# Gated graph layers on one core: dense superblocks of 16 quads whose sums land in two spans of 256 columns

## The chip, the cores and the metric

The kernel runs on one core of a Trainium2 chip. The metric is the time of one execution on the device, in microseconds (us); the lower, the better. The kernel before was run three times: median 3903.62 us, from 3901.79 to 3904.91. A fourth execution was profiled.

## What is computed

A graph of 12500 nodes with 128 features and 212500 edges, sorted by destination, goes through three gated graph layers:

```python
h = x @ lin_w.T + lin_b            # x here: relu of the layer norm of the input
for i in range(3):
    m = h @ weight[i]
    agg = segment_sum(m[src], dst, n_nodes)
    h = gru_cell(agg, h, w_ih, w_hh, b_ih, b_hh)
return x_in + h
```

The sum over edges is the expensive part: each of 212500 edges adds a row of 128 numbers of `m` to the row of its destination.

## The kernel before, in words

**Edges.** 512 consecutive edges are a quad: 4 chunks (`QC`) of 128. There are 416 quads. As the edges are sorted by destination, a quad touches few nodes: its destinations lie in a window of `W` = 36 nodes from its lowest one. Sums are kept transposed in `aggT`, features on the partitions and nodes along the columns, so a quad adds 36 columns at a column known only on the chip. VectorE makes a plan first (lines 971 to 1050): the lowest node of every quad, the edges' distances to it, and flags that say whether every edge lies in its window. All engines wait for the flags and then take one of two written orders of work. With these inputs it is the first (`TILES_AT`, `AHEAD`).

**Two ways to sum.** The quads are cut in 16 superblocks of `SQ` = 26 consecutive quads. In each layer a superblock's last `GQ` = 12 quads are gathered and its first `DQ` = 14 are dense.
- *Gathered* (a step is two quads): GpSimd issues eight indirect DMAs, one a chunk (line 565), that bring 128 message rows each, in three bf16 pieces, into a ring of 4 steps. TensorE multiplies them with onehots that VectorE makes (24 small matmuls, line 827), and VectorE adds the two windows into `aggT` (line 1174), its columns from registers loaded from the plan.
- *Dense*: no message is gathered. For a superblock there is a matrix of counts, source nodes by columns: how many edges go from a source to each of a quad's 36 window columns. Its product with all messages of the 12544 source nodes (98 blocks of 128) gives all 14 windows at once, 14 x 36 = 504 columns of PSUM (lines 846 to 865). The messages are split by VectorE in two fp32r halves (lines 1283, 1285), so there are 98 x 2 matmuls a superblock. The counts come from HBM as bytes, a slice of 7 blocks per DMA (line 509), and ScalarE widens them (line 682). Work is cut in units of 2, 2 and 3 blocks (`UNITS`), 42 a superblock; two slices of six units in all are buffered (`UBUF`).

**The counts** are made once, in layer 0, where the first `KG` = 7 superblocks are gathered whole (91 steps, `TURN`). For every one of 16 x 14 = 224 dense quads VectorE makes onehots of its sources (lines 1241, 1249), and in 7 rounds of 14 blocks (`ROUNDS`) TensorE counts with 4 matmuls (line 842) into one of three banks of PSUM. ScalarE writes the bank as bytes into `quad_counts` (`evacuate`, line 709), and SP stores 7 quads, half a superblock, with 7 DMAs (line 515), each as soon as the last quad's round has left PSUM. The next superblock's same half waits for these stores. After all stores SP loads the first counts and messages (lines 509, 501). From step 91 on layer 0 sums its other 9 superblocks half dense, half gathered.

**Order.** Each engine runs the steps of a layer in a written order (`layer_steps`): 145, 96 and 96 steps. On TensorE a step is: the sums of the gathered rows, the next messages of a tile (256 nodes), the counting rounds or seven dense units (`STEP_UNITS`), and the gates of a tile when all its sums are in (`TILES_AT`). On VectorE: the two adds of the step, onehots, parts of tiles, then in turn the splitting of units and, once a superblock's last unit is multiplied, `add_superblock`: 14 adds of 36 columns (line 1188), each waiting on the one before, seven register loads before each seven. The gathers of the next layer wait until all messages of a layer are stored; dense units of its first parts are done ahead, in the steps after a layer's last gather.

The change touches also the loads (`counts_in`), the layout of the counts in HBM, and what TensorE waits for (`s_dadd`: the adds of a superblock two back, in whose bank it writes).

## Time and profile before

| | |
|---|---|
| median of 3 runs | 3903.62 us |
| profiled execution: its own time | 3896.86 us |
| profiled execution: span, first to last instruction | 3895.0 us |
| mean granted TensorE clock | 0.952 |
| TensorE matmuls, busy | 3452.6 us, 89% |
| ScalarE, busy | 3020.0 us, 78% |
| VectorE, busy | 2870.7 us, 74% |
| GpSimd, busy | 2756.7 us, 71% |
| DMA | 758.66 MB, 195 GB/s |

In the rows PE is TensorE's matmuls, PEld its weight loads, DVE VectorE, ACT ScalarE, POOL GpSimd, SP the sync engine; an engine's name with q is its sequencer. L565 is line 565 of the kernel before. The span falls in stages: the plan and the first messages up to about 157 us, gathers with counting up to about 1130, a gap until the first counts are back at about 1195, the dense part of layer 0 until 1818, layer 1 until 2892, layer 2 until the end. Granted clock is the share of 2.4 GHz that TensorE was given: 1.0, or 0.5 (1.2 GHz), and means between them over a stretch.

### The profile page before, as it was taken

The page shows a single profiled execution, that of the slowest core. Times are in us where ns is not written, and L with a number is a line of the kernel's source. Part 1 is how long each engine was busy: PE and PEld are TensorE (multiplying, and loading weights), DVE is VectorE, ACT ScalarE, POOL GpSimd, SP SyncE. Part 2 cuts the span into 40 slices and gives each one's busy share as a digit, 9 for nine tenths or more (in the row PEclk, how much of TensorE's full clock was granted, in tenths as well). Part 3 has the DMA queues.
Part 4 walks back from the last instruction along what each step waited for, and adds up shares of the span by engine and source line. Part 5 has one row for each costly group of instructions (what it writes and reads, how often), then busy time and mean ns, then how long its engine had stood idle before and what let it go on. Part 6 is the DMA issues. An engine that isn't in the chain of part 4 may idle for free.

```text
span 3895.0 us, 74412 instructions
## 1 busy us (share of the span) xinstructions
PE 3452.6 (89%) x25008; PEld 2729.5 (70%) x25009; DVE 2870.7 (74%) x8189; ACT 3020.0 (78%) x4231; POOL 2756.7 (71%) x2758
## 2 busy tenths in 40 slices
PE   6289999999979999987999999999979999999996
PEld 4167666766667777765777777777757777777775
DVE  7478888888867777765777777777757777777774
ACT  4179888888878888776788788787857887878783
POOL 4777777777777777733777777777737777777776
PEclk8699999999989999998999999999989999999998
DMA  8346566565577666665666666666756666666664
GB/s 274 108 152 216 187 197 208 185 200 196 180 240 235 192 198 198 191 183 169 194 204 199 198 202 207 192 205 191 227 159 191 205 197 196 204 194 202 194 201 121
DMA packets 461502, 758.66 MB, mean 195 GB/s; under 512 B 66760, under 2 KB 337864, under 8 KB 461128
## 3 DMA queue, kind: packets, MB, share of 16 engines
q1 hardware_dynamic: 216472, 411.54, 33.0%
q0 software_dynamic: 129408, 265.20, 24.6%
q10 hardware_dynamic: 115248, 77.10, 6.4%
q8 instruction: 213, 3.49, 0.4%
q14 instruction: 161, 1.32, 0.1%
HBM read 578.11 MB, written 175.47 MB: 193 GB/s over the span
## 4 chain that ended last, share of the span: by engine, by line
PE 43%; POOL 23%; DVE 11%; issue 10%; ACT 7%; DMA 4%; DVEq 2%; ACTq 0%; SPq 0%; POOLq 0%
POOL ring_region L565 23%; PE psum L860 18%; PE psum L842 16%; ACT wide_counts L682 4%; DVE quad_onehots L1249 2%; PE psum L815 2%; PE psum L827 2%; DMA states<-temps 2%; DVE aggT L1188 2%; DVEq L1140 2%; DVE message_halves L1285 1%; PE psum L785 1%; PE psum L786 1%; PE psum L787 1%; ACT quad_counts L709 1%
## 5 line engine op out<-in xcount | busy, mean ns | idle before, releaser
L565 POOL DMA_INDIRECT ring_region<-messages,edge_src x2696 | 2702.7, 1002 | 1048.7 <-issue 804.2
L860 PE MATMUL psum<-wide_counts,message_halves 128*128 128x504 f32 x8036 | 1988.3, 404 | 149.7 <-DVE message_halves L1285 129.7
L682 ACT CAST wide_counts<-messages_region 128x1008 fp32r<-128x1008 uint8 x1722 | 1880.7, 1170 | 257.9 <-PE psum L860 202.6
L860 PEld LDWEIGHTS psum<-wide_counts,message_halves 128*128 128x128 f32 x8036 | 1517.0, 192 | 516.5 <-ACT wide_counts L682 111.9
L1285 DVE TENSOR_TENSOR message_halves<-messages_region,message_halves 128x256 fp32r<-128x256 f32 x1722 | 810.9, 471 | 59.3
L842 PE MATMUL psum<-quad_onehots,block_onehots 128*128 128x238 bf16 (+2 forms) x6272 | 768.3, 272 | 60.6 <-ACT quad_counts L709 42.4
L709 ACT CAST quad_counts<-psum 128x504 uint8<-128x504 f32 x1568 | 770.6, 643 | 28.5 <-PE psum L842 26.5
L842 PEld LDWEIGHTS psum<-quad_onehots,block_onehots 128*128 128x128 bf16 x6272 | 539.7, 100 | 276.4 <-issue 47.6
L1283 DVE CAST message_halves<-messages_region 128x256 fp32r<-128x256 f32 x1722 | 656.7, 381 | 64.0 <-PE psum L860 35.2
L1249 DVE TENSOR_SCALAR quad_onehots<-iota_quad,count_keys 128x1666 bf16<-128x1666 f16 (+2 forms) x896 | 528.3, 652 | 0.0
L827 PEld LDWEIGHTS psum<-onehot,ring_region 128*128 128x128 bf16 x8088 | 243.4, 96 | 187.2 <-issue 160.3
L827 PE MATMUL psum<-onehot,ring_region 128*128 128x36 bf16 x8088 | 258.2, 179 | 129.6 <-DMA ring_region<-messages,edge_src 122.2
L1174 DVE TENSOR_TENSOR aggT<-aggT,psum 128x36 f32 x674 | 128.3, 190 | 227.6 <-PE psum L827 100.1
L1241 DVE TENSOR_SCALAR block_onehots<-iota_block,count_keys 128x128 bf16<-128x128 bf16 x896 | 171.6, 274 | 108.1 <-PE psum L842 107.3
L1188 DVE TENSOR_TENSOR aggT<-aggT,psum 128x36 f32 x574 | 110.7, 193 | 182.3 <-issue 88.9
L627 ACT ACTIVATE temps<-psum,small 128x256 f32<-128x256 f32 x147 | 69.2, 471 | 211.7 <-PE psum L815 211.2
L815 PE MATMUL psum<-aggT,wih 128*128 128x256 f32 x882 | 219.4, 386 | 10.6 <-DVE aggT L1188 10.6
L1217 DVE SCALAR_TENSOR_TENSOR temps<-psum,small,temps 128x256 f32<-128x256 f32 x147 | 70.6, 480 | 196.7 <-ACT temps L627 188.7
L815 PEld LDWEIGHTS psum<-aggT,wih 128*128 128x128 f32 x882 | 172.1, 195 | 36.2 <-issue 11.4
L637 ACT ACTIVATE temps<-temps,small 128x256 f32<-128x256 f32 x147 | 75.1, 511 | 127.3 <-DVE temps L1219 127.1
L1149 DVE TENSOR_TENSOR onehot<-iota_block,edge_rel 128x288 bf16<-128x288 bf16 x337 | 152.1, 452 | 1.7 <-DVE count_keys L1070 0.9
L665 ACT CAST pieces_out<-temps 128x256 bf16<-128x256 f32 x98 | 41.7, 426 | 139.1 <-DVE temps L1196 139.1
(104 smaller groups left out, 1529.3 us busy)
## 6 DMA issues: line engine op xcount, KB each, us to landing
messages_region<-counts SPq DMA_DIRECT2D x574, 441.0 KB
counts<-quad_counts SPq DMA_DIRECT2D x224, 441.0 KB
ring_region<-messages,edge_src POOLq DMA_INDIRECT x2696
messages<-pieces_out ACTq DMA_DIRECT2D x98, 192.0 KB
messages_region<-plain SPq DMA_DIRECT2D x21, 896.0 KB, 7.6
temps<-states ACTq DMA_DIRECT2D x98, 128.0 KB
states<-temps ACTq DMA_DIRECT2D x98, 128.0 KB
plain<-temps ACTq DMA_DIRECT2D x98, 128.0 KB
```

The costliest lines, as they stand in the source:

```text
L565: nc.gpsimd.indirect_dma_start(out=rows[:, n % RING, h * QC + c, :], out_offset=None, in_=messages[layer], in_offset=bass.IndirectOffsetOn ...
L682: nc.scalar.copy(wide_counts[:, v % UBUF, :, cols], stage[v % ABUF][:, :, cols]).then_inc(s_wide, 1)
L709: nc.scalar.copy(quad_counts[half][:, 2 * i:2 * i + 2, j % HQ, :], psum[:, COUNT_BANKS[r % 3], 0:RW].rearrange("p (s w) -> p s w", w=SLW)) ...
L815: nc.tensor.matmul(bank, wih[:, gate * P:(gate + 1) * P], nodes, start=alone, stop=True, skip_group_check=not alone).then_inc(s_gate, 1)
L827: mm = nc.tensor.matmul(window(n, h), rows[:, n % RING, i, k * P:(k + 1) * P], onehot[:, n % 3, i, :], start=(c == 0 and k == 0), stop=(c ...
L842: mm = nc.tensor.matmul(by_block[:, :, SUBLOW[c]:SUBLOW[c] + SUBW[c]], blocks_oh[j % 2][:, c, :], x_round, start=(k == 0), stop=True, skip ...
L860: mm = nc.tensor.matmul(psum[:, 6 + kg % 2, 0:DQ * W], halves[:, v % UBUF, b % HB, half * P:(half + 1) * P], wide_counts[:, v % UBUF, :, c ...
L1188: nc.vector.tensor_tensor(cols, cols, psum[:, 6 + kg % 2, q * W:(q + 1) * W], ALU.add).then_inc(s_dadd, 1)
L1241: made = nc.vector.tensor_scalar(blocks_oh[j % 2][:, c, :], iota_lo[:], los[:, col:col + 1], None, ALU.is_equal)
L1249: made = nc.vector.tensor_scalar(xs[j % 2][c], iota_x[:, 0:NB * SUBW[c]], keys[:, col:col + 1], -float(SUBLOW[c]), ALU.subtract, ALU.is_equal)
L1283: nc.vector.tensor_copy(high, whole).then_inc(s_high, 1)
L1285: nc.vector.tensor_tensor(low, whole, high.bitcast(F32), ALU.subtract).then_inc(s_low, 1)
```

## The change

Superblocks have 28 quads, 16 of them dense; there are 15, the last one short of 4 gathered quads (`CUT` = 2 steps). The 16 dense quads of a superblock are two halves of 8. The 8 windows of a half share one span of `WW` = 256 columns that starts at the lowest node of its first quad, so a dense matmul has 2 x 256 columns, and a superblock's sums are added with two adds of 256 columns.

For that the counts of a quad are put in place when they leave PSUM: ScalarE writes them into `half_counts` (98 blocks of 264 bytes) at the quad's offset in the span. The offsets are a third row of the plan, loaded into registers of ScalarE eight at a time. Windows overlap: a quad leaves its column 0 alone when it isn't the first of a half, as this node may be shared with the quad before, and an extra round (two matmuls of 98 columns, one of them with `shared_onehots`) counts that column for both quads; ScalarE copies it in as 98 single bytes. VectorE clears the tail of a half beforehand. The plan gets new conditions (gaps between quads, offsets, edges beyond the next quad) and one more onehot key per quad (`shared_keys`). Stores wait for a whole half. `blocks_oh` gets a third buffer.

```diff
-SQ = 26
-DQ = 14
+SQ = 28
+DQ = 16
 GQ = SQ - DQ
 HB = 7
 HQ = DQ // 2
-SLW = HB * W
+WW = 256
+WS = 264
+LAST_FROM, LAST_TO = WS - 2 * W, WS - W
 RW = 2 * HB * W
...
 SUBW = (12, 19, 17, 17)
+SUBFROM = (0, 1, 11, 19)
...
-FIRST_DENSE = 9 / 16
+FIRST_DENSE = 8 / 15
...
-    NSB = NQ // SQ
-    AGG = NODES + W
-    assert NPAD % (PTN * PRO) == 0 and NQ % SQ == 0 and out.shape[0] % TN == 0 and NB % (2 * HB) == 0
+    NSB = -(-NQ // SQ)
+    QUADS = NSB * SQ
...
-    STEPS = [TURN + KD * GSB, G_STEPS, G_STEPS]
-    STEP0 = [0, STEPS[0], STEPS[0] + G_STEPS]
+    STEPS = [TURN + KD * GSB - CUT, G_STEPS - CUT, G_STEPS - CUT]
+    STEP0 = [0, STEPS[0], STEPS[0] + STEPS[1]]
     TOTAL = sum(STEPS)
     BUILDS = NSB * DQ
-    BUILD_ROUNDS = BUILDS * ROUNDS
+    COUNTED = [(j, i) for j in range(BUILDS) for i in range(ROUNDS + (j % HQ > 0))]
+    COUNTED_AT = {round_of: e for e, round_of in enumerate(COUNTED)}
+    COUNTED_BY = [max(e for e, (quad, _) in enumerate(COUNTED) if quad == j) + 1 for j in range(BUILDS)]
...
+                whole = s == STEPS[layer] - 1 and (not ahead or layer == LAYERS - 1)
+                now = end if whole else min(block_of(unit_of(d) + STEP_UNITS), max(d, end))
...
+            half_counts_t = shared("half_counts", [P, 2, NB, WS], U8)
-            blocks_oh_t = shared("block_onehots", [P, 2, QC, P], BF16)
+            blocks_oh_t = shared("block_onehots", [P, 3, QC, P], BF16)
+            shared_oh_t = shared("shared_onehots", [P, 2, NB], BF16)
...
-        wide_counts = sb("wide_counts", [P, UBUF, DQ, HB * W], F32R)
+        wide_counts = sb("wide_counts", [P, UBUF, HB, 2, WW], F32R)
...
-        stage = [byte_at(region, ST0 + b * AB, DQ * SLW, U8).rearrange("p (q w) -> p q w", w=SLW)
+        stage = [byte_at(region, ST0 + b * AB, AB, U8).rearrange("p (h b w) -> p b h w", h=2, w=WS)
...
+        counts_tail = [half_counts_t[:, half].bitcast(F32)[:, :, LAST_TO // 4:WS // 4] for half in range(2)]
...
-                sp.dma_start(stage[v % ABUF], counts[k, j]).then_inc(s_al[v % ABUF], 16)
+                sp.dma_start(stage[v % ABUF].rearrange("p b h w -> p h b w"), counts[k, j]).then_inc(s_al[v % ABUF], 16)
 
             for g in range(BUILDS // HQ):
                 k, half = BUILD_ORDER[g // 2], g % 2
+                sp.wait_ge(s_ev, COUNTED_BY[HQ * g + HQ - 1])
                 for i in range(ROUNDS):
-                    sp.wait_ge(s_ev, ROUNDS * (HQ * g + HQ - 1) + i + 1)
-                    sp.dma_start(counts[k, 2 * i:2 * i + 2, :, HQ * half:HQ * (half + 1), :].rearrange(
-                        "s p q w -> p s (q w)"), quad_counts[half][:, 2 * i:2 * i + 2].rearrange(
-                        "p s q w -> p s (q w)")).then_inc(s_ast[half], 16)
+                    sp.dma_start(counts[k, 2 * i:2 * i + 2, :, half].rearrange("s p b w -> p s (b w)"),
+                                 half_counts[half][:, 2 * HB * i:2 * HB * (i + 1), :].rearrange(
+                                     "p (s b) w -> p s (b w)", b=HB)).then_inc(s_ast[half], 16)
...
-                cols = slice(*(W * b for b in UNITS[w % UN]))
+                here = slice(*UNITS[w % UN])
                 if w % UN == 0:
                     act.wait_ge(s_al[v % ABUF], 16 * (v // ABUF + 1))
                 unit_used(act, w - UBUF * UN)
-                nc.scalar.copy(wide_counts[:, v % UBUF, :, cols], stage[v % ABUF][:, :, cols]).then_inc(s_wide, 1)
+                nc.scalar.copy(wide_counts[:, v % UBUF, here], stage[v % ABUF][:, here, :, 0:WW]).then_inc(s_wide, 1)
...
+                j, i = COUNTED[e]
                 k, half = j // DQ, j % DQ // HQ
-                act.wait_ge(s_bld, r + 1)
-                if k and j % HQ == 0 and i == 0:
-                    act.wait_ge(s_ast[half], 16 * ROUNDS * k)
-                nc.scalar.copy(quad_counts[half][:, 2 * i:2 * i + 2, j % HQ, :],
-                               psum[:, COUNT_BANKS[r % 3], 0:RW].rearrange("p (s w) -> p s w", w=SLW)).then_inc(s_ev, 1)
+                if j % HQ == 0 and i == 0:
+                    first = DQ * BUILD_ORDER[k] + HQ * half
+                    _, values = nc.values_load_multi_w_load_instructions(
+                        plan[0:1, 2, first:first + HQ], [mybir.EngineType.Activation], min_val=0, max_val=LAST_TO,
+                        skip_runtime_bounds_check_because=ON_CHIP)
+                    columns.update((j + q, value) for q, value in enumerate(values))
+                    act.wait_ge(s_tail, j // HQ + 1)
+                    if k:
+                        act.wait_ge(s_ast[half], 16 * ROUNDS * k)
+                act.wait_ge(s_bld, e + 1)
+                counted = psum[:, COUNT_BANKS[e % 3], :]
+                if j % HQ:
+                    act.wait_ge(s_ev, COUNTED_AT[j - 1, min(i, ROUNDS - 1)] + 1)
+                if i < ROUNDS:
+                    own = 1 if j % HQ else 0
+                    nc.scalar.copy(half_counts[half][:, 2 * HB * i:2 * HB * (i + 1), own:WS][
+                                       :, :, bass.ds(columns[j], W - own)],
+                                   counted[:, 0:RW].rearrange("p (b w) -> p b w", w=W)[:, :, own:W]).then_inc(s_ev, 1)
+                else:
+                    nc.scalar.copy(half_counts[half][:, :, bass.ds(columns[j], 1)],
...
+                if i == ROUNDS:
+                    pe.wait_ge(s_xshare, j - j // HQ)
+                    first_column = xs[j % 2][0].rearrange("p (b w) -> p b w", w=SUBW[0])[:, :, 0]
+                    nc.tensor.matmul(counted[:, 0:NB], blocks_oh[j % 3][:, 0, :], first_column, start=True, stop=False)
+                    nc.tensor.matmul(counted[:, 0:NB], blocks_oh[(j - 1) % 3][:, QC - 1, :], shared_oh[j % 2],
+                                     start=False, stop=True).then_inc(s_bld, 1)
+                    return
...
-                    pe.wait_ge(s_dadd, DQ * (kg - 1))
-                cols = slice((b % HB) * W, (b % HB + 1) * W)
+                    pe.wait_ge(s_dadd, 2 * (kg - 1))
                 for half in range(HALVES):
-                    mm = nc.tensor.matmul(psum[:, 6 + kg % 2, 0:DQ * W],
+                    mm = nc.tensor.matmul(psum[:, 6 + kg % 2, 0:2 * WW],
                                           halves[:, v % UBUF, b % HB, half * P:(half + 1) * P],
-                                          wide_counts[:, v % UBUF, :, cols], start=(b == 0 and half == 0),
+                                          wide_counts[:, v % UBUF, b % HB].rearrange("p h w -> p (h w)"),
+                                          start=(b == 0 and half == 0),
                                           stop=(b == NB - 1 and half == HALVES - 1))
...
+            dense_low = dense_quads(lowest_all)
+            nc.vector.memset(gap[:, NQ - 1:NQ], float(FAR)).then_inc(s_win, 1)
+            nc.vector.tensor_tensor(gap[:, 0:NQ - 1], lowest[:, 1:NQ], lowest[:, 0:NQ - 1], ALU.subtract
+                                    ).then_inc(s_win, 1)
+            for half in range(2):
+                quads = slice(HQ * half, HQ * (half + 1))
+                nc.vector.tensor_tensor(offsets[:, :, quads], dense_low[:, :, quads],
+                                        dense_low[:, :, HQ * half:HQ * half + 1].to_broadcast([P, NSB, HQ]),
+                                        ALU.subtract).then_inc(s_win, 1)
...
+            nc.vector.tensor_tensor(beyond_c[:, :, 0:QC - 1], by_quad[:, :, 0:QC - 1],
+                                    limit_of.to_broadcast([P, NQ, QC - 1]), ALU.is_ge).then_inc(s_win, 1)
...
+            nc.vector.tensor_tensor(outside, outside, beyond, ALU.max).then_inc(s_win, 1)
...
+            near_next = chunk_of(edge_rel[:], QC - 1, SQ)[:, :, 0:DQ - 1]
+            nc.vector.tensor_tensor(shared_keys[:, :, 1:DQ], near_next, dense_quads(gap_all)[:, :, 0:DQ - 1], ALU.is_equal
+                                    ).then_inc(s_keys, 1)
...
-                    count = DQ // 2
-                    values = lows_of(SQ * k + half * count, count)
-                    for j in range(count):
-                        q = half * count + j
-                        cols = aggT[:, bass.ds(values[j], W)]
-                        if kg or q:
-                            dve.wait_ge(s_dadd, DQ * kg + q)
-                        nc.vector.tensor_tensor(cols, cols, psum[:, 6 + kg % 2, q * W:(q + 1) * W], ALU.add
-                                                ).then_inc(s_dadd, 1)
+                    value, = lows_of(SQ * k + HQ * half, 1)
+                    cols = aggT[:, bass.ds(value, WW)]
+                    if kg or half:
+                        dve.wait_ge(s_dadd, 2 * kg + half)
+                    nc.vector.tensor_tensor(cols, cols, psum[:, 6 + kg % 2, WW * half:WW * (half + 1)], ALU.add
+                                            ).then_inc(s_dadd, 1)
...
+                k, half = j // DQ, j % DQ // HQ
+                if j % HQ == 0:
+                    if k:
+                        dve.wait_ge(s_ast[half], 16 * ROUNDS * k)
+                    nc.vector.memset(counts_tail[half], 0.0).then_inc(s_tail, 1)
                 block_onehot(j)
+                if j % HQ:
+                    nc.vector.tensor_scalar(shared_oh[j % 2], iota_hi[:, 0:NB], shared_keys[:, BUILD_ORDER[k], j % DQ:j % DQ + 1],
+                                            None, ALU.is_equal).then_inc(s_xshare, 1)
```

## Rows read from the trace of the kernel before

**Rows 1.** The page: busy time of the engines, and the chain by engine.
```profile
PE 3452.6 (89%) x25008; PEld 2729.5 (70%) x25009; DVE 2870.7 (74%) x8189; ACT 3020.0 (78%) x4231; POOL 2756.7 (71%) x2758
...
PE 43%; POOL 23%; DVE 11%; issue 10%; ACT 7%; DMA 4%; DVEq 2%; ACTq 0%; SPq 0%; POOLq 0%
```

**Rows 2.** Costliest groups, dense stretches of layer 0, 1 (two), 2: busy, mean ns | idle.
```profile
L860 PE MATMUL psum<-wide_counts,message_halves 128*128 128x504 f32 x1593 | 392.2, 402 | 38.8 <-DVE message_halves L1285 38.7
...
L565 POOL DMA_INDIRECT ring_region<-messages,edge_src x673 | 667.5, 992 | 221.2 <-issue 200.1 <-PE psum L827 21.1
L860 PE MATMUL psum<-wide_counts,message_halves 128*128 128x504 f32 x2660 | 667.1, 408 | 53.0 <-DVE message_halves L1285 52.7
...
L860 PE MATMUL psum<-wide_counts,message_halves 128*128 128x504 f32 x2980 | 727.4, 400 | 29.3 <-DVE message_halves L1285 27.9 <-ACT wide_counts L682 1.3
```

**Rows 3.** Stretches: length, busy PE, PEld, DVE, ACT, POOL, clock, DMA, GB/s.
```profile
205.00:1125.00 920.00, 859.42 (x8494) 639.52 (x8493) 777.06 (x2163) 810.64 (x1689) 699.06 (x680) 0.99 0.60 193
1195.00:1730.00 535.00, 496.15 (x3153) 401.32 (x3152) 390.85 (x1112) 428.55 (x509) 366.49 (x370) 0.96 0.66 193
...
1892.00:2780.00 888.00, 833.25 (x5284) 676.17 (x5281) 652.07 (x1866) 718.57 (x857) 667.12 (x673) 0.96 0.67 199
...
2895.00:3840.00 945.00, 895.68 (x5794) 726.53 (x5794) 711.59 (x2025) 755.28 (x771) 722.87 (x730) 0.99 0.66 196
```

**Rows 4.** Counting: a piece of the chain (start, us), and costliest groups.
```profile
383.57 9.02 PE psum L842 x76
...
L709 ACT CAST quad_counts<-psum 128x504 uint8<-128x504 f32 x1552 | 762.4, 644 | 27.7 <-PE psum L842 25.9
L842 PE MATMUL psum<-quad_onehots,block_onehots 128*128 128x266 bf16 (+1 forms) x6214 | 760.1, 272 | 60.6 <-ACT quad_counts L709 42.4 <-DVE quad_onehots L1249 17.8
```

**Rows 5.** Timeline of layer 1 (start, us, what), and a stretch as in rows 3.
```profile
2141.32 7.65 PE L860 MATMUL psum<-wide_counts,message_halves 128*128 128x504 f32 x32
...
2162.76 2.14 DVE L1188 TENSOR_TENSOR aggT<-aggT,psum 128x36 f32 x7 [1.37 <-PE psum L860]
...
2166.66 2.13 DVE L1188 TENSOR_TENSOR aggT<-aggT,psum 128x36 f32 x7 [1.76 <-issue]
...
2169.62 3.38 PE L860 MATMUL psum<-wide_counts,message_halves 128*128 128x504 f32 x8 [4.20 <-DVE message_halves L1285]
...
2169.60:2176.00 6.40, 5.76 (x19) 4.24 (x20) 5.45 (x16) 4.44 (x5) 4.87 (x6) 0.73 0.46 132
```

**Rows 6.** The plan on VectorE: groups, then the timeline after 120 us.
```profile
L1017 DVE TENSOR_TENSOR messages_region<-messages_region 128x416 f32<-128x416 f32 x4 | 3.4, 889 | 0.1
...
L998 DVE TENSOR_TENSOR edge_rel<-edge_rel,messages_region 128x1664 f32<-128x1664 f32 x1 | 1.9, 1867 | 0.0
...
123.44 1.36 POOL L565 DMA_INDIRECT ring_region<-messages,edge_src  x1 [0.21 <-issue]
...
157.17 0.52 DVE L1174 TENSOR_TENSOR aggT<-aggT,psum 128x36 f32 x2 [0.73 <-PE psum L827]
...
172.95 0.52 DVE L1174 TENSOR_TENSOR aggT<-aggT,psum 128x36 f32 x2 [9.14 <-PE psum L827]
```

**Rows 7.** Operations of 256 columns from PSUM, over the span.
```profile
L1219 DVE TENSOR_TENSOR temps<-temps,psum 128x256 f32<-128x256 f32 x147 | 61.8, 421 | 5.1
...
L655 ACT COPY temps<-psum 128x256 f32<-128x256 f32 x98 | 35.2, 359 | 11.2 <-PE psum L798 11.2
```

**Rows 8.** The last stores of counts: their issue, and the last one's landing.
```profile
1131.31 6.88 SPq L515 DMA_DIRECT2D counts<-quad_counts  x7
...
1136.98 7.46 DMA counts<-quad_counts
```

**Rows 9.** TensorE at the ends of layers 0 and 1.
```profile
1748.05 2.90 PE L815 MATMUL psum<-aggT,wih 128*128 128x256 f32 x6 [9.49 <-DVE aggT L1188]
...
1818.06 0.88 PE L827 MATMUL psum<-onehot,ring_region 128*128 128x36 bf16 x24 [17.71 <-DMA ring_region<-messages,edge_src]
...
2892.25 0.88 PE L827 MATMUL psum<-onehot,ring_region 128*128 128x36 bf16 x24 [16.36 <-DMA ring_region<-messages,edge_src]
```

143 lines of the change are left out of this document (104 added, 39 removed).

## The prediction, made before the change was run

> **What bounds the kernel now.** I read the engines' busy shares first, then the chain of waits, then the span cut at the kernel's stages, then each stage's costliest lines. TensorE is busiest, and the chain is TensorE 43% and GpSimd 23% [rows 1]: two engines share the bound. GpSimd does nothing but issue gathers, one per 0.99 + 0.30 us [rows 2], so a step of eight costs 10.3 us and six steps (one superblock) 61.9 us, whatever the others do.
>
> By stage [rows 3] (a superblock is 196 dense matmuls):
> - 205 to 1125: counting. 224 quads in 920 us, 4.11 us a quad. Per quad TensorE is busy 3.84 us, ScalarE 3.62, VectorE 3.47: TensorE bounds and ScalarE is close behind, and TensorE's largest wait is for ScalarE's evacuation [rows 4].
> - 1195 to 1730: layer 0's dense part, 1593 matmuls are 8.13 superblocks: 65.8 us each. Layer 1, from 1892 us on, 2660 are 13.57: 65.4 us each. Layer 2, 2980 are 15.2: 62.2 us each [rows 2, 3]. Layer 2 therefore already goes at the gathers' pace. Layers 0 and 1 don't, and the reason is in the waits: TensorE waits for VectorE's halves 38.7, 52.7 and 27.9 us in the three stretches.
> - One such wait from close by [rows 5]: VectorE makes 14 adds of 36 columns, each waiting for the one before, in two groups with register loads between, from 2162.76 to 2168.79: 6.0 us in which it splits no messages. TensorE runs out and idles 4.2 us. Then the granted clock of the next 6.4 us is 0.73: between the levels 2.4 and 1.2 GHz, part of it at the lower, where a dense matmul takes 0.42 us (8 in 3.38) against 0.24 (32 in 7.65). The granted clock over the stretch is 0.96 in layers 0 and 1, 0.99 in layer 2 [rows 3], that is 2.6 us lost per superblock in the first two and 0.6 in the last.
>
> **The change, part by part.** From the constants: 16 superblocks of 26 quads become 15 of 28, the number of gathered quads in one stays 12. The last superblock is short by 4 gathered quads (2 steps). Steps go from 145, 96, 96 to 144, 88, 88; dense superblocks over all layers from 41 to 38; counted quads from 224 to 240, their rounds from 1568 to 1680, with 210 small extra rounds for the shared column.
>
> *Plan.* Some 18 more VectorE instructions stand before the flags. By rows of like size [rows 6]: one over 1664 elements 1.9 us, one over three quarters of them 1.4, four over strided 416 at 0.89, and a dozen over fewer elements, each below that, which I estimate at 3 together: 10 us. The three on the shared keys add 1. TensorE sums nothing until then, but the gathers run: the first is issued at 123.4, the ring of four steps is full 32 gathers of 1.3 us later, at 165, and the adds soon come at the gathers' pace (the one at 172.95 after 9.1 us of waiting for sums). The first add moves 11 us, from 157 to 168, so the gathers stall some 3 us. **+3**; without that cover it would be +11, and nothing less than 0.
>
> *Counting, TensorE.* A quad gets two matmuls of 98 columns for 7 of 8 quads. Nineteen rounds (76 matmuls of 227 columns on average) take 9.02 us, 0.119 each [rows 4]; 98 columns save 129/2.4 = 54 ns: 0.065 each, 0.13 a quad. Ends: 0, hidden in ScalarE's time, and 0.24. Busy becomes 3.97 us a quad.
>
> *Counting, ScalarE.* The evacuation of 504 columns lasts 644 ns and, overlapping, costs 0.49 each. It now writes 14 runs of 35 bytes at a column held in a register, and waits for its own earlier result. No such write is in the trace; the nearest is VectorE's add at a register's column that waits for the one before, 0.305 us apart, under 0.49 [rows 5]. So I take 0.49 (lower end 0.48 for 14 columns fewer; upper end 0.644, no overlap). The extra copy of 98 columns: from 644 ns at 504 and 359 at 256 [rows 4, 7], 1.15 ns a column, 0.18 us; upper end a whole 0.49. Register loads, eight a half: seven took 1.76 us on VectorE [rows 5], so 0.25 us a quad; lower end 0 if they run ahead. Together 3.62 + 0.18 + 0.25 = 4.05 us a quad: ScalarE passes TensorE.
>
> *Counting, VectorE.* One onehot of 98 columns (0.2) and, per 8 quads, a clearing of 882 elements (0.9 us, 0.11 a quad): 3.78 us a quad. It stays under the others and costs nothing while they are slower; uncovered it would be 0.3 a quad. The clearing waits for the stores of the same half; behind it in VectorE's queue are adds and onehots. It comes two quads ahead of use, some 26 us after that half's last count, and the last stores of a half landed 7.5 us after issue [rows 8]: covered.
>
> *Sum.* A quad took 0.27 us more than its busiest engine; with two engines nearly level I allow 0.30: 4.35 us, 240 quads 1044 us against 920: **+124**. Ends: loads hidden, 4.10, +64; every evacuation unoverlapped, under the rivals.
>
> *The turn.* Seven stores now wait in SP's queue for the whole half, where six went out while the last quad was still counted; behind them are all the loads. The seven were issued over 6.9 us and the last landed 7.5 later, and the first load followed [rows 8]. Nearly all of those 6.9 us come after the last count now: **+6**, between 0 and 12.
>
> *Dense superblocks.* 14 serial adds with their loads become 2 of 256 columns: an add of 256 columns with PSUM 0.42 us [rows 7], with its load 0.3 more, 1.4 us instead of 6 to 7. TensorE has six units in hand then (14 blocks, 28 matmuls, 6.7 us), so the wait goes, and with it most of the clock's fall. Per superblock: stall 4.8 us in layer 0 and 3.9 in layer 1, of which I take 3.2 to 4.0; clock 2.1; against it 196 matmuls 8 columns wider, 196 x 3.3 ns = 0.65, and 0.2 more of a tile, of the 11 us that sums and tiles take on TensorE per superblock (895.7 less 727.4 over 15.2 in layer 2), at most 0.9. TensorE's need falls to 61 us, level with the gathers' 61.9. Two engines level don't meet exactly: 63. Widening grows by 1.6%, on ScalarE, which is busy 81% of layer 1 [rows 3], beside TensorE. The tiles, the loads (532 of 473 KB for 574 of 441 KB) and the gathers are as before.
> - Layer 0: one superblock fewer, 7.13 at 63 = 449 for 535, -86; the layer's last tiles waited 9.5 us for the last adds [rows 9], now 3: -6; two gather steps fewer, 1 us of sums each: -2. **-94**.
> - Layer 1, 1818 to 2892 [rows 9]: 1074 = 16 x 65.4 + 28. Now 88 steps, 14.67 superblocks at 63 = 924, + 28, + 10 since 33 dense blocks (15.7 us, a third hidden by the wait for the next gathers) stand beside the last two tiles. 962: **-112**.
> - Layer 2: 1003 = 16 x 62.2 + 8. The gathers' pace stays: 14.67 x 62.2 = 912, + 8, + 3 for one more tile at the end: **-80**.
>
> Sum: 3 + 124 + 6 - 94 - 112 - 80 = **-153**. Against the profiled execution (span 3895.0, its own time 3896.9) this gives a span of 3742 and a time of 3744. The median of the three runs is 3903.6, 6.8 above it: **3751 us**, -3.9%.
>
> **The rivals.**
> *R1, the evacuation becomes the bound (slower).* If writes at a register's column in short runs, or the new wait on ScalarE's own semaphore, keep evacuations from overlapping, each costs its 644 ns: 4.51 + 0.18 + 0.25 + 0.18 = 5.12 us of ScalarE a quad, with 0.30 5.42, 240 quads 1300, 256 more than forecast: 4007 us. It decides from 0.583 us an evacuation on (153 us / 240 = 0.64 a quad). For it: ScalarE is 94% as busy as TensorE already, and layer 0 alone pays. Against: the wait is for a result seven evacuations old, and the register-addressed adds pass at 0.305.
> *R2, the one-column copies are dear.* They write 98 single bytes 264 apart and TensorE reads a column 12 elements apart. If a copy costs what an evacuation of 504 does, 0.31 more x 210 = 65 us: 3816. For it: nothing in the trace writes so thinly. Against: the copies are few.
> The Trainium skill (SBUF — State Buffer, Door 1) speaks for R2: SBUF has 16-byte cachelines and each access that crosses to a new line pays a penalty. It gives no price for ScalarE, and no run here shows one.
> *R3, another wait takes the place.* The stall and the clock's loss stay in other clothes (ScalarE's widening, 81% busy in layer 1 [rows 3], or late gathers), and only the count of superblocks pays: layer 0 7.13 x 65.8 = 469, -66 - 8; layer 1 14.67 x 65.4 + 38 = 997, -77; layer 2 -80. -231 + 133 = -98: 3806.
> *R4, the plan refuses.* If the new conditions on gaps and offsets failed for these node numbers, the flags would send all engines to the order with tiles last. Sums and tiles take TensorE 168 us in layer 2 [rows 2, 3], now among the dense work; alone after the steps they would add up to that in each layer: up to 4250. Destinations are sorted and quads 30 nodes wide, which fits 256 columns for 8.
>
> **Chances and range.** Forecast 0.57, R2 0.15, R3 0.16, R1 0.11, R4 0.01. About 0.2% is what a measurement here can tell from no change (the three runs span 0.08%). R2 and R3 with other shortfalls reach no change in 0.03. So faster 0.85, within 0.2% 0.03, slower 0.12. Low end: loads hidden, 3751 - 60, near 3695. High end: R2 and R3 together, 3871. R1 and R4 are left out.
>
> **What the profile would show.** Gathers 2560; dense matmuls 7448 at 0.24; adds of 256 columns 76; TensorE's wait for message halves under 30 us over the span (129.7 now) and the granted clock 0.98 or more in layer 1. Counting lasts some 1045 us with ScalarE over 90% busy in it, evacuations near 0.49 apart. Layer 1 and 2 take about 962 and 923 us. I am wrong if an evacuation costs 0.58 or more, if TensorE in layer 1 waits as long for something else, or if layer 2 isn't shorter by 80.

## The result, and the profile after

The changed kernel takes **3806.20 us** (median of four runs, 3801.6 to 3813.78) where the kernel before took 3904.26 on the same chip: a ratio of 0.9749, 95% interval 0.9737 to 0.9761, so 2.5% faster. The forecast was 3751, -3.9%, with a range from 3695 to 3871. The direction held; 55 us of the 153 did not come.

The page of the changed kernel, busy time by engine and the chain of waits, stands beside [rows 1]:

```profile
PE 3361.6 (88%) x24880; PEld 2652.7 (70%) x24881; DVE 2801.6 (74%) x7778; ACT 3044.4 (80%) x4427; POOL 2663.4 (70%) x2622
...
POOL 35%; PE 23%; issue 15%; ACT 15%; DVE 6%; DMA 4%; ACTq 1%; DVEq 0%; SPq 0%; POOLq 0%
```

Over the whole span PE, POOL and DVE do less, since there are fewer superblocks. ScalarE does more, in a shorter span, and its share of the chain went from 7% to 15%. TensorE's share fell from 43% to 23% and GpSimd's rose from 23% to 35% [rows 1]: the gathers now lead the chain.

The costliest groups of the page (line, engine, operation, tiles and shape, count | busy, mean ns | idle before it and what ended it):

```profile
L600 POOL DMA_INDIRECT ring_region<-messages,edge_src x2560 | 2609.2, 1019 | 1037.5 <-issue 764.2
L717 ACT CAST wide_counts<-messages_region 128x1024 fp32r<-128x1024 uint8 (+1 forms) x1596 | 1762.0, 1185 | 188.5 <-PE psum L920 155.1
L920 PE MATMUL psum<-wide_counts,message_halves 128*128 128x512 f32 x7448 | 1794.4, 398 | 70.3 <-DVE message_halves L1406 50.5
...
L903 PE MATMUL psum<-quad_onehots,block_onehots 128*128 128x266 bf16 (+1 forms) x6720 | 844.7, 272 | 104.2 <-ACT half_counts L758 63.8
L758 ACT CAST half_counts<-psum 128x490 f32 (+1 forms) x1680 | 846.9, 594 | 64.6 <-PE psum L903 40.2
L903 PEld LDWEIGHTS psum<-quad_onehots,block_onehots 128*128 128x128 bf16 x6720 | 576.4, 100 | 359.5 <-issue 137.0
...
L1354 DVE TENSOR_SCALAR block_onehots<-iota_block,count_keys 128x128 bf16<-128x128 bf16 x960 | 183.6, 271 | 137.9 <-PE psum L896 101.4
...
L762 ACT CAST half_counts<-psum 128x98 f32 x210 | 128.1, 610 | 0.0
```

Gathers (2560) and dense matmuls (7448) are as counted, and TensorE's wait for message halves is 50.5 us for 129.7. New is the last row: L762 is the one-column copy, **610 ns** for 98 bytes, as long as an evacuation of 490. And L903's weight loads stand 137 us for "issue", time for which the profile names no releaser; run 4 looks into a part of it.

The stretches of the changed kernel, as in [rows 3] (length, busy PE, PEld, DVE, ACT, POOL, granted clock, DMA share, GB/s): counting, then the dense parts of layers 0, 1 and 2.

```profile
206.00:1300.00 1094.00, 989.97 (x9550) 715.58 (x9551) 884.71 (x2568) 958.17 (x2018) 787.39 (x736) 0.99 0.52 167
1372.00:1800.00 428.00, 407.28 (x2681) 335.01 (x2680) 318.93 (x867) 367.69 (x441) 307.63 (x308) 1.00 0.71 209
1898.00:2814.00 916.00, 866.96 (x5678) 712.62 (x5675) 679.55 (x1826) 780.37 (x926) 693.87 (x695) 0.99 0.72 213
2872.00:3740.00 868.00, 824.79 (x5352) 679.96 (x5349) 641.48 (x1710) 701.07 (x716) 664.20 (x669) 0.98 0.68 202
```

The clock of layers 0 and 1 rose from 0.96 to 1.00 and 0.99. In the counting stretch TensorE is busy 90% and ScalarE 88% (forecast: over 90%): neither of the two is saturated.

To compare stage by stage I cut both spans at the starts of VectorE's adds of gathered steps, which every kernel here has (us; in brackets us per step):

| stage | before | after | difference | forecast |
|---|---|---|---|---|
| to the add of step 6 | 202.9 | 206.1 | +3 | +3 |
| counting, to two steps before the turn | 931.3 | 1104.1 | **+173** | +124 |
| turn, six steps | 62.6 | 62.6 | 0 | +6 |
| layer 0, dense steps | 535.3 (10.92) | 427.9 (10.44) | -107 | |
| layer 0's last add to layer 1's first | 87.0 | 97.7 | +11 | -94 with the line above |
| layer 1, steps | 1037.6 (10.92) | 915.6 (10.53) | -122 | |
| its last add to layer 2's first | 36.6 | 58.2 | **+22** | -112 with the line above |
| layer 2, steps | 986.4 (10.38) | 904.5 (10.40) | -82 | |
| end | 15.4 | 25.2 | +10 | -80 with the line above |
| span | 3895.0 | 3802.1 | -93 | -153 |

The dense stages did what was forecast, within 3 to 12 us each (layer 0 -97, layer 1 -100, layer 2 -72). Four fifths of the shortfall of 60 us of span (49) are in the counting; 12 more are at the turn from layer 1 to layer 2.

### The profile page after: what moved, and what is told of

It is laid out like the page before. It is cut to its first block, busy times and chain, and to the rows that moved or that the text cites. A ratio compares the mean times of both kernels' runs of the same rounds, so it can differ in the third digit from the quotient of the medians.

```text
span 3802.1 us, 76920 instructions
## 1 busy us (share of the span) xinstructions
PE 3361.6 (88%) x24880; PEld 2652.7 (70%) x24881; DVE 2801.6 (74%) x7778; ACT 3044.4 (80%) x4427; POOL 2663.4 (70%) x2622
## 4 chain that ended last, share of the span: by engine, by line
POOL 35%; PE 23%; issue 15%; ACT 15%; DVE 6%; DMA 4%; ACTq 1%; DVEq 0%; SPq 0%; POOLq 0%
POOL ring_region L600 34%; PE psum L903 16%; ACT wide_counts L717 10%; ACT half_counts L758 3%; DMA states<-temps 2%; DVE quad_onehots L1370 2%; PE psum L920 2%; PE psum L880 1%; PE psum L868 1%; DVE block_onehots L1354 1%; PE psum L811 1%; DVE temps L1330 1%; DMA messages_region<-counts 1%; PE psum L804 0%; ACTq L745 0%
## 5 line engine op out<-in xcount | busy, mean ns | idle before, releaser
L717 ACT CAST wide_counts<-messages_region 128x1024 fp32r<-128x1024 uint8 (+1 forms) x1596 | 1762.0, 1185 | 188.5 <-PE psum L920 155.1
L920 PE MATMUL psum<-wide_counts,message_halves 128*128 128x512 f32 x7448 | 1794.4, 398 | 70.3 <-DVE message_halves L1406 50.5
L920 PEld LDWEIGHTS psum<-wide_counts,message_halves 128*128 128x128 f32 x7448 | 1397.6, 191 | 374.8 <-ACT wide_counts L717 90.0
L903 PE MATMUL psum<-quad_onehots,block_onehots 128*128 128x266 bf16 (+1 forms) x6720 | 844.7, 272 | 104.2 <-ACT half_counts L758 63.8
L758 ACT CAST half_counts<-psum 128x490 f32 (+1 forms) x1680 | 846.9, 594 | 64.6 <-PE psum L903 40.2
L903 PEld LDWEIGHTS psum<-quad_onehots,block_onehots 128*128 128x128 bf16 x6720 | 576.4, 100 | 359.5 <-issue 137.0
L1406 DVE TENSOR_TENSOR message_halves<-messages_region,message_halves 128x256 fp32r<-128x256 f32 (+1 forms) x1596 | 751.0, 471 | 55.0
L1404 DVE CAST message_halves<-messages_region 128x256 fp32r<-128x256 f32 (+1 forms) x1596 | 611.4, 383 | 114.1 <-PE psum L920 75.7
L1370 DVE TENSOR_SCALAR quad_onehots<-iota_quad,count_keys 128x1176 bf16<-128x1176 f16 x960 | 560.7, 645 | 0.0
L1290 DVE TENSOR_TENSOR aggT<-aggT,psum 128x36 f32 x640 | 122.2, 191 | 216.4 <-PE psum L880 147.8
L762 ACT CAST half_counts<-psum 128x98 f32 x210 | 128.1, 610 | 0.0
```

The costliest lines, as they stand in the source:

```text
L717: nc.scalar.copy(wide_counts[:, v % UBUF, here], stage[v % ABUF][:, here, :, 0:WW]).then_inc(s_wide, 1)
L758: nc.scalar.copy(half_counts[half][:, 2 * HB * i:2 * HB * (i + 1), own:WS][:, :, bass.ds(columns[j], W - own)], counted[:, 0:RW].rearrange ...
L903: mm = nc.tensor.matmul(by_block[:, :, SUBLOW[c]:SUBLOW[c] + SUBW[c]], blocks_oh[j % 3][:, c, :], x_round, start=(k == 0), stop=True, skip ...
L920: mm = nc.tensor.matmul(psum[:, 6 + kg % 2, 0:2 * WW], halves[:, v % UBUF, b % HB, half * P:(half + 1) * P], wide_counts[:, v % UBUF, b % ...
L1370: made = nc.vector.tensor_scalar(xs[j % 2][c], iota_x[:, 0:NB * SUBW[c]], keys[:, col:col + 1], -float(SUBLOW[c]), ALU.subtract, ALU.is_equal)
L1404: nc.vector.tensor_copy(high, whole).then_inc(s_high, 1)
```

## Experiments

Every kernel ran with the kernel before on the same chip, three rounds and more. The ratios are to that kernel; the edits are to the changed kernel, or to the folded one where this is said.

**1. Registers taken out.** ScalarE's columns are constants, the 240 register loads go. The counts are put at 30 columns a quad instead of where they belong.

```diff
-                    _, values = nc.values_load_multi_w_load_instructions(...)
-                    columns.update((j + q, value) for q, value in enumerate(values))
+                    columns.update((j + q, 30 * q) for q in range(HQ))
...
-                                       :, :, bass.ds(columns[j], W - own)],
+                                       :, :, columns[j]:columns[j] + W - own],
...
```

> The kernel after, but ScalarE writes every quad at a constant column (30 per quad) instead of the plan's: no register loads on ScalarE and no register in the address. Counts stand up to some columns off their place, so the sums are not the reference's; the work is the same. Theory A (the counting lost its 49 us to the one-column rounds, not to registers): the eight loads a half are seen as some 17 us of idle, the time falls by 10 to 25 us to 3780-3796, evacuations stay 0.48 us apart. Rival B (writes at a register's column are slow): the spacing falls to 0.42-0.46 us and the time by 60 us or more, below 3746.

3770.31 us, ratio 0.9661 (0.9642 to 0.9681): 36 us less. Counting 1071.8 for 1104.1; evacuations start 471 ns apart for 479. More than theory A wrote down, and the spacing didn't fall as B wanted. The traces show one part of it: with a column from a register an evacuation starts 97 ns after TensorE's signal that its round is done, with a constant one 23 ns (medians). What costs more, the load or the address, is taken up in runs 8 to 10.

**2. The copy made cheap.** The one-column copy moves a single byte instead of 98; the other counts of the first columns are left out.

```diff
-                    nc.scalar.copy(half_counts[half][:, :, bass.ds(columns[j], 1)],
-                                   counted[:, 0:NB].unsqueeze(2)).then_inc(s_ev, 1)
+                    nc.scalar.copy(half_counts[half][:, 0:1, bass.ds(columns[j], 1)],
+                                   counted[:, 0:1].unsqueeze(2)).then_inc(s_ev, 1)
```

> The kernel after, but the copy of the shared column moves 1 element instead of 98 single bytes 264 apart; the rounds on TensorE stay. 97 of 98 blocks keep no count in the shared columns. Theory A1 (each single byte is dear, 4 to 5 ns): from this copy's start to the next evacuation's start goes from 0.48 to 0.1-0.25 us, ScalarE is freed of 50-75 us, and the time falls by 20 to 45 us, since TensorE's own 0.52 us per extra round stays. Rival A2 (the cost is fixed, whatever is copied): the spacing stays above 0.4 us and the time within 10 us of 3806.

3809.42 us, ratio 0.9748 (0.9726 to 0.9770): the time of the changed kernel. The copy did become cheap. The groups on ScalarE from 206 to 1240 us, and under them the stretch itself and ScalarE's longest wait in it, of this kernel:

```profile
L762 ACT CAST half_counts<-psum 128x1 f32 x195 | 35.2, 180 | 0.0
...
206.00:1240.00 1034.00, 933.36 (x8992) 685.83 (x8991) 833.29 (x2414) 843.57 (x1902) 716.02 (x694) 0.98 0.52 165
...
ACT half_counts L758 <- PE psum L903: 96.5, 244, 2.4
```

and of the changed kernel:

```profile
206.00:1240.00 1034.00, 935.26 (x9033) 675.52 (x9034) 837.66 (x2433) 907.46 (x1911) 746.49 (x697) 0.99 0.52 167
...
ACT half_counts L758 <- PE psum L903: 38.6, 65, 1.9
```

ScalarE is busy 64 us less and waits 58 us longer for TensorE: what it saved it waits. From the copy's start to the next evacuation's start are 480 ns as before, so A1's gain didn't come although the copy fell to 180 ns, as A1 had it. As long as the extra round stands on TensorE, the bytes of the copy are not what the counting goes by. So rival R2's mechanism falls, though its time (3816) was near.

**3. The serial adds put back.** Sixteen adds of 32 columns a superblock, each waiting on the one before, in place of two of 256 (the sums land at 32 columns a quad from the half's lowest node).

```diff
-                    value, = lows_of(SQ * k + HQ * half, 1)
-                    cols = aggT[:, bass.ds(value, WW)]
-                    if kg or half:
-                        dve.wait_ge(s_dadd, 2 * kg + half)
-                    nc.vector.tensor_tensor(cols, cols, psum[:, 6 + kg % 2, WW * half:WW * (half + 1)], ALU.add
-                                            ).then_inc(s_dadd, 1)
+                    values = lows_of(SQ * k + HQ * half, HQ)
+                    for j in range(HQ):
+                        q = HQ * half + j
+                        cols = aggT[:, 32 * j:AGG][:, bass.ds(values[0], 32)]
+                        if kg or q:
+                            dve.wait_ge(s_dadd, DQ * kg + q)
+                        nc.vector.tensor_tensor(cols, cols, psum[:, 6 + kg % 2, 32 * q:32 * (q + 1)], ALU.add
+                                                ).then_inc(s_dadd, 1)
```

> The kernel after, but a superblock's sums are added by 16 serial adds of 32 columns, with eight register loads before each eight, as the kernel before did with 14 of 36; same sums. Theory C (the dense stages gained by the stall and the clock that these adds cost, beside the fewer superblocks): TensorE's wait for message halves comes back to 100 us or more over the span from 50, the granted clock in layer 1 falls from 0.99 to 0.96, a superblock in layers 0 and 1 goes from 62.9 to 65.5 us or more, and the time rises by 50 to 90 us to 3856-3896. Rival D (only the smaller number of superblocks paid): within 15 us of 3806.

3865.52 us, ratio 0.9901 (0.9884 to 0.9917): 59 us more, three fifths of all that the change won. Per step, layer 0 10.98 for 10.44, layer 1 10.92 for 10.53, layer 2 10.38 for 10.40. Layer 1, dense matmuls and the stretch, of this kernel:

```profile
L920 PE MATMUL psum<-wide_counts,message_halves 128*128 128x512 f32 x2683 | 661.3, 403 | 54.9 <-DVE message_halves L1408 54.1 <-ACT wide_counts L717 0.8
...
1898.00:2814.00 916.00, 832.25 (x5343) 678.59 (x5342) 674.23 (x1932) 742.94 (x885) 682.42 (x684) 0.96 0.69 203
```

and the same group of the changed kernel:

```profile
L920 PE MATMUL psum<-wide_counts,message_halves 128*128 128x512 f32 x2847 | 685.1, 397 | 26.9 <-DVE message_halves L1406 26.9
```

With the adds back the wait for halves doubles (over the whole span it is 96.1 us for 50.5, a little under the 100 of theory C), the clock is 0.96 as before [rows 3], and 164 fewer matmuls get done in the same 916 us. Layer 2 doesn't change: it goes at the gathers' pace either way.

**4. The shared column folded in.** Instead of an extra round of two matmuls of 98 columns and a copy, each of the seven rounds adds the neighbour's share of its own 14 first columns with a fifth matmul of 14 columns, and the evacuation writes all 36 columns. Nothing of the counts is left out.

```diff
-    COUNTED = [(j, i) for j in range(BUILDS) for i in range(ROUNDS + (j % HQ > 0))]
+    COUNTED = [(j, i) for j in range(BUILDS) for i in range(ROUNDS)]
...
-                    own = 1 if j % HQ else 0
+                    own = 0
...
+                if j % HQ:
+                    mm = nc.tensor.matmul(by_block[:, :, 0], blocks_oh[(j - 1) % 3][:, QC - 1, :],
+                                          shared_oh[j % 2][:, 2 * HB * i:2 * HB * (i + 1)],
+                                          start=False, stop=True, skip_group_check=True)
                 mm.then_inc(s_bld, 1)
```

> The kernel after with the extra round folded in: in each of a quad's 7 rounds a fifth matmul of 14 columns adds the previous quad's shared node into column 0 in PSUM, ScalarE writes all 36 columns, and there is no separate round and no one-column copy. Theory A (the extra round costs ScalarE 0.49 and TensorE 0.52 us a quad): the counting stage goes from 1104 us to 1010-1050 and the time falls by 50 to 95 us to 3711-3756. Rival E (the counting stage is held by VectorE's onehots or the gathers): the stage stays above 1085 us and the time within 20 us of 3806.

3749.55 us, ratio 0.9606 (0.9590 to 0.9622): **57 us** less than the changed kernel, counting 1053.9 for 1104.1. The timeline of the changed kernel shows the price. TensorE in it, two quads (start, length, line, operation, count):

```profile
350.73 0.33 PE L895 MATMUL psum<-quad_onehots,block_onehots 128*128 128x98 bf16 x1
350.88 0.22 PE L896 MATMUL psum<-shared_onehots,block_onehots 128*128 128x98 bf16 x1
351.26 3.42 PE L903 MATMUL psum<-quad_onehots,block_onehots 128*128 128x266 bf16 x28
354.52 0.33 PE L895 MATMUL psum<-quad_onehots,block_onehots 128*128 128x98 bf16 x1
354.68 0.23 PE L896 MATMUL psum<-shared_onehots,block_onehots 128*128 128x98 bf16 x1
```

From L895 to L896 are 0.15 us, from L896 to the next round's first matmul 0.38 (medians over some 170 quads 0.155 and 0.362; between two matmuls of a round 0.111). An extra round takes TensorE 0.52 us from start to start.

The 0.36 are a wait for ScalarE. Ahead of each round TensorE waits (line 890) until the bank of three rounds before is emptied. The same place in the chain of waits, and another such place in the timeline:

```profile
350.49 0.63 ACT half_counts L758
351.12 0.14 issue
351.26 1.80 PE psum L903 x14
...
1301.66 0.22 PE L896 MATMUL psum<-shared_onehots,block_onehots 128*128 128x98 bf16 x1
1302.03 3.43 PE L903 MATMUL psum<-quad_onehots,block_onehots 128*128 128x266 bf16 x28 [0.15 <-ACT half_counts L758]
```

Of 168 extra rounds with a counting round right behind them, 28 have no such wait on record, and there the next round starts after 0.065 us. In 133 of the other 140 it starts 56 or 57 ns after the record of the wait ends, and an evacuation ended the wait. ScalarE in turn starts most evacuations 97 ns after a round of TensorE has ended (median), and gives the copy a whole slot of 0.48 (the median from L762 to the next L758, and the same from one L758 to the next). So the banks go round in a ring in which each engine waits for the other, and the extra round is one more turn of it. The bank that TensorE waits for behind an extra round is that of an evacuation and not the copy's, which fits with run 2 having won nothing. No run relieves TensorE alone, so its share and the copy's aren't told apart.

**5. No extra round at all.** Only the first two edits of run 4: the neighbour's share of a first column is left out.

> The changed kernel without the 210 extra rounds: the share that a quad's neighbour adds to its first column is left out, each quad evacuates all its columns itself. Theory A: an extra round cost TensorE 0.52 us start to start (0.123 + 0.155 + 0.362 less one ordinary matmul start of 0.12), 210 of them 109 us, and all of it was on the path: counting 1104 to 995, time 3697 (3680 to 3715). Rival B: ScalarE's spacing of 0.48 us an evacuation takes over before that: 1680 of them 806, 240 register loads of 0.25 us 60, and the tile work and idle time beside them as in the folded kernel: counting 1030 to 1050, time 3733 to 3752, so that nothing of the folded kernel's gain is left to be had from the fifth matmuls.

3746.81 us, ratio 0.9607 (0.9585 to 0.9628), counting 1047.2: the folded kernel's ratio within 0.0001. Rival B in place and size: the 1470 small matmuls of the folded kernel cost nothing that can be seen, and evacuations start 483 ns apart. But it isn't ScalarE alone that sets this pace: most evacuations still start 96 ns after TensorE's round ended, and most rounds 56 ns after the wait for a bank. Here a round's first matmul starts 182 ns after the fourth one of the round before; in the folded kernel the fifth matmul stands in that wait, 108 ns after the fourth, and the next round starts 80 ns after it (medians of the rounds with a wait on record). So the extra rounds and their copies cost 55 to 59 us in the changed kernel (by ratio and by time), and folding gives all of it back. VectorE makes the onehots of the shared column in both kernels, so their cost isn't in this.

**6. Layer 1's tail.** The 33 dense blocks beside layer 1's last two tiles go behind its last messages, into one step more.

```diff
-        return range(max(tiles_at) + 1 + low_lag(layer, max(tiles_at)))
+        return range(max(tiles_at) + 1 + low_lag(layer, max(tiles_at)) + (layer == 1))
...
+                if ahead and layer == 1 and s >= STEPS[1]:
+                    if s <= max(TILES_AT[1]) + 2:
+                        end = d
+                    else:
+                        at[layer, s] = range(d, ends[1] + 70)
+                        d = ends[1] + 70
+                        continue
```

> The changed kernel with the 33 dense blocks that the plan put beside layer 1's last two tiles moved behind its last messages, where TensorE waits for layer 2's first gathers. Theory A: those blocks and their widenings stand between the last gates and messages, so the stretch from layer 1's last add to layer 2's first one falls from 58.2 to 42 to 47 us, and the time from 3806 to 3791 to 3797. Rival B: the stretch is set by the last tile's own chain (gates, state, messages, store, gather) however the blocks lie: 55 to 59 us, time 3803 to 3809. Rival C: the widenings behind the last store now hold ScalarE when layer 2 begins and what the tail gains layer 2 gives back: tail 42 to 47, layer 2 904 to 915, time 3801 to 3809.

3788.03 us, ratio 0.9711 (0.9684 to 0.9737), against 0.9749 for the changed kernel. The stretch from add to add fell from 58.2 to 47.5, layer 2's steps took 901.6 for 904.5. That is theory A's place; its sizes (42 to 47, 3791 to 3797) are missed by 0.5 us and by 3. TensorE's timeline of the changed kernel (in brackets the idle time before, and its releaser):

```profile
2826.62 7.62 PE L920 MATMUL psum<-wide_counts,message_halves 128*128 128x512 f32 x32
...
2836.93 6.74 PE L920 MATMUL psum<-wide_counts,message_halves 128*128 128x512 f32 x28
2844.54 1.62 PE L920 MATMUL psum<-wide_counts,message_halves 128*128 128x512 f32 x6 [0.88 <-DVE message_halves L1406]
2846.01 0.60 PE L851 MATMUL psum<-wmsg,temps 128*128 128x128 f32 x4
2852.21 1.19 PE L851 MATMUL psum<-wmsg,temps 128*128 128x128 f32 x4 [5.60 <-DVE temps L1309]
2871.27 0.88 PE L880 MATMUL psum<-onehot,ring_region 128*128 128x36 bf16 x24 [17.87 <-DMA ring_region<-messages,edge_src]
```

and of this one:

```profile
2828.59 0.68 PE L858 MATMUL psum<-wmsg,temps 128*128 128x128 f32 x4
2833.58 1.20 PE L858 MATMUL psum<-wmsg,temps 128*128 128x128 f32 x4 [4.30 <-DVE temps L1316]
2834.43 17.17 PE L927 MATMUL psum<-wide_counts,message_halves 128*128 128x512 f32 x66
2855.95 0.88 PE L887 MATMUL psum<-onehot,ring_region 128*128 128x36 bf16 x24 [4.35 <-DMA ring_region<-messages,edge_src]
```

The same 66 matmuls (32, 28 and 6 of them in the first fence) stood ahead of the last messages while TensorE later idled 17.9 us for the first gathers; behind the messages they fill that idle time. The last messages come 24.1 us after layer 1's last add instead of 38.1, and the gathers start earlier; 3.3 of these 14.0 us are lost again until the first gathered rows are summed.

**7. Both, and layer 0's tail too.** The folded kernel with run 6's edit:

> Both edits that won time in one kernel: the shared column folded into the rounds, and layer 1's last 33 dense blocks behind its last messages. They act in different stages (counting in layer 0, the turn from layer 1 to layer 2), so their gains add if nothing links them: theory A: the folded kernel's 3749.6 less the 11 us of layer 1's tail and the 3 us that layer 2 ran shorter = 3736 (3731 to 3742). Rival B: the tail's gain was partly the scatter of its runs: 3742 to 3750.

3731.45 us (3729.98 to 3735.46), ratio **0.9560** (0.9545 to 0.9576): the gains add. With the 21 blocks beside layer 0's last tile moved as well:

> The same, and in layer 0 the 21 dense blocks beside its last tile moved behind its last messages. Theory A: as in layer 1, blocks and widenings beside the last tile cost about 5 us a tile (10.7 us for two), so layer 0's tail falls from 97.7 to 91 to 94 and the time by 4 to 7 more than with layer 1 alone: 3730 (3725 to 3735). Rival B: layer 0's last tile is set by its own chain of gates and products, and nothing is won: tail 96 to 99, time as the kernel with layer 1's tail alone.

3731.11 us, ratio 0.9551 (0.9532 to 0.9570). Layer 0's tail did fall, from 97.2 to 93.5, the 4 us of theory A, but the time of the whole can't be told from the kernel with layer 1's tail alone: the intervals overlap nearly whole. It stays open whether those 4 us are lost elsewhere or in the scatter; in the profiled executions the counting, which the edit doesn't touch, differs by 8.

**8. Folded, without registers.** Run 1's edit on the folded kernel (the counts are misplaced again).

> The folded kernel (a fifth matmul of 14 columns in each round, no round of its own for the shared column) without the register loads: the counts of every quad land at constant columns 30 apart, so they are misplaced. Theory A: the loads and register addresses on ScalarE cost what they cost in the run with fixed columns alone, 32 to 36 us of counting, also here: counting 1054 to about 1020, time 3749.6 - 36 = 3714 (3700 to 3728). Rival B: with the fifth matmul in every round TensorE is now the bound of counting and ScalarE's loads lie beside it: under 15 us, 3735 to 3750.

3717.17 us, ratio 0.9527 (0.9507 to 0.9546), counting 1018.2: 32 us less than the folded kernel, theory A. Once the extra rounds are gone ScalarE's registers cost as much as before.

**9. Loads one by one.** In the folded kernel each load stands ahead of its own quad.

> The folded kernel with the eight register loads of a half taken one by one, each ahead of its quad's first evacuation, instead of all eight ahead of the first. Theory A: a burst of eight loads (2 us by 0.25 us each) outlasts the three counting banks, and single loads hide behind a round of TensorE: half or more of the 36 us is won, 3720 to 3735. Rival B: each load costs ScalarE its 0.25 us on the path wherever it stands: 3745 to 3753.

3756.92 us, ratio 0.9630 (0.9609 to 0.9651): nothing won, rather 7 us lost, though the intervals still overlap. It is rival B's direction, a little beyond its range. Scattering the loads doesn't hide them; they are 0.28 us each in the records (282 ns of TENSOR_LOAD) against 0.55 for the whole burst of eight.

**10. Loads or addresses?** The folded kernel with constant columns, its loads left in the source:

> The folded kernel with its register loads left in, but the counts put at constant columns 30 apart (misplaced): the 240 loads remain, the addresses from registers go. Theory A: the loads are the cost (8 in a burst, 30 bursts): time near the folded kernel's, counting 1045 to 1054, 3742 to 3752. Rival B: forming the address of each of 1680 evacuations from a register is the cost (479 to 471 ns, 8 ns each, 13 us, and more where it stands between wait and start): counting 1018 to 1030, 3717 to 3728. In between, both.

3718.27 us, ratio 0.9528 (0.9510 to 0.9547). That looked like rival B, but the trace has no TENSOR_LOAD left on ScalarE's sequencer: with their values unused the loads had gone too, so this was run 8 once more. The next kernel keeps them in use, in the last of a quad's seven evacuations:

> The folded kernel in which one evacuation of a quad in seven takes its column from the register and six take constant columns 30 apart (misplaced), so that the register loads stay in the program while six of seven address formings go. In the run before this one the loads had gone from the trace with the addresses (no TENSOR_LOAD record on ScalarE's sequencer), so it did not tell the two apart. Folded kernel 3749.6, without both 3717. Theory A: the loads cost the idle time put down to issue before the evacuations (15.2 us in the folded kernel, 0.5 without loads) and a drained ring behind each burst, the greater part of the 33: 3735 to 3746, issue idle 12 to 16. Rival B: the addresses are the greater part: 3719 to 3730, spacing of evacuations 476 to 478 ns.

3738.60 us, ratio 0.9579 (0.9564 to 0.9594). Between the folded kernel's 0.9606 and 0.9527 of run 8 this is a third of the way. What one line waits for, of ScalarE's evacuations from 206 to 1240 us, in this kernel:

```profile
L758 ACTq ALU_OP  x238: 35/35/51, 212.7 to 1237.9; - x119
...
  issue: 12.2, 9
```

in the folded kernel (L758) and without registers (L754):

```profile
L758 ACTq ALU_OP  x1650: 35/35/53, 210.1 to 1239.9; - x184
...
  issue: 15.2, 9
```

```profile
engine op xcount: duration ns min/median/max, first and last start us, forms
L754 ACT CAST half_counts<-psum x1680: 556/642/712, 211.1 to 1223.2; 128x504 uint8<-128x504 f32 x187
...
  issue: 0.5, 2
```

Each address is an ALU_OP of 35 ns on the sequencer ahead of its evacuation. Six sevenths of them gone win some 11 us (0.0027 of 3901); the loads with the last seventh make up the other 20 or so, of which 12 show as ScalarE's idle time put down to issue. Theory A by the time and by the idle time put down to issue: the loads are the greater part. The split is rough, as this kernel's interval overlaps the folded one's by 0.0004, and the distance of the evacuations (475 ns) doesn't help: it is even below what rival B wrote.

## Why the prediction was right or wrong

**What bounds, and the dense part: right.** "The wait goes, and with it most of the clock's fall": the wait for halves fell from 129.7 to 50.5 us over the span (forecast under 30, so not all of it), the clock of layer 1 is 0.99 (forecast 0.98 or more), the adds of 256 columns take 0.42 us each as forecast, and a superblock takes six steps of 10.44 and 10.53 us, 62.6 and 63.2, for a forecast of 63. Run 3 shows the cause: the adds alone are worth 59 us and bring wait and clock back. R3 wrote a time of 3806, exactly what came out, and is wrong all the same: no wait took the stall's place.

**Layer 2: right in its reason**, the gathers' pace: 10.40 us a step, and unmoved by the adds in run 3. The 82 us come from eight steps fewer. The end grew by 10 where the sum had 3 for one more tile. So layer 2 with its end is 72 us shorter; by the prediction's own sign ("isn't shorter by 80") it misses, by those tiles and not by its pace.

**Layers 0 and 1 in sum: -97 for -94, -100 for -112.** The 12 are layer 1's tail, 22 longer than before where the sum had "+10 since 33 dense blocks stand beside the last two tiles". The blocks were priced rightly: run 6 moves them and wins 10.7. What the sum put at nothing are the tiles themselves. Behind the last add TensorE makes the gates of three tiles where the kernel before made those of one. At the end of layer 2, where no dense block stands, this shows alone; of the kernel before, and then of the changed one:

```profile
3884.95 2.43 PE L815 MATMUL psum<-aggT,wih 128*128 128x256 f32 x6
...
3779.22 1.82 PE L868 MATMUL psum<-aggT,wih 128*128 128x256 f32 x6
...
3783.66 1.46 PE L868 MATMUL psum<-aggT,wih 128*128 128x256 f32 x6
...
3787.91 1.46 PE L868 MATMUL psum<-aggT,wih 128*128 128x256 f32 x6
```

That end grew by 10 us, and layer 1's tail without its blocks (run 6) is 47.5 us for 36.6, 11 more. No run changes the tiles alone, so this is read from the stages and not tried. The wait for the next gathers, 17.9 us, is no shorter than the 16.4 of before [rows 9].

**The counting: the step that failed, +173 for +124.** The argument took a quad's time as the busiest engine's plus 0.30, and let ScalarE's new work first use up its 0.22 us of slack under TensorE. Against the 4.16 us a quad of before (931.3 / 224) it is now 4.60 (1104.1 / 240), 0.44 more. By part:
- *The extra round on TensorE* was priced by its columns, 0.065 us a matmul. It takes the engine 0.52 us, of which 0.36 are the wait for ScalarE's bank, which the columns can't tell. *The copy on ScalarE* was priced at 0.18 by its columns; it takes a slot of 0.48. Without both the counting is 50 us shorter in run 4 and 57 in run 5, 0.21 to 0.24 a quad. The sum had the copy at 0.18 a quad less slack.
- *Registers* were priced at 0.25 us a quad, 60 us, lower end 0; without them the counting is 32 us shorter in run 1 and 36 in run 8, 0.14 a quad. The load was overpriced and the address on each evacuation not priced at all.
- *The evacuation itself* was right: 0.49 expected, 0.48 measured. R1 falls: writes in short runs at a column from a register overlap like the others.
- With both out (run 8) a quad takes 4.24 us, so they are 0.36 of the 0.44. The other 0.08 a quad, 20 us, wasn't tried. VectorE's shared onehot (263 ns, forecast 0.2) and its clearing (793 ns, forecast 0.9) are candidates: VectorE's `quad_onehots` make 15.9% of the chain from 206 to 1240 us in run 8, where they made 10.6% from 205 to 1125 in the kernel before.

The sum set against slack is what was wrong: of 0.43 us added on ScalarE, 0.24 were to show. TensorE and ScalarE hand three banks round, and what holds a bank on either engine reaches the other, as the waits beside run 4 show; slack in busy time doesn't take it up. How much of it was taken up all the same wasn't tried.

**R2** had its condition met (the copy costs what an evacuation does) and its time nearly right, 3816. But its cause, the thin bytes, isn't what the time goes by: with one byte the copy fell to 180 ns and the kernel stayed where it was. That the time is near is luck. The Trainium skill (SBUF — State Buffer, Door 1) has it that an access that crosses to a new 16-byte line pays a penalty. The rows agree in kind: 98 bytes on 98 lines took 430 ns more than one byte, 4.4 ns for each further one, where an evacuation is at 0.85 ns by the same reckoning (594 ns for 490 in runs of 35).

**Plan and turn.** The first add came 15 us later (171.9 for 157.2) for a forecast of 11, and the gathers in hand covered all but 3.3, as forecast. At the turn the stores were indeed issued together and late: the first dense matmul comes 23.0 us after the last counts have left PSUM where it came 18.5 after that before, 4.4 of the 6 forecast. But the adds of the gathered steps around it went on at the gathers' 10.4 us a step, so the stage cost nothing.
